# A two-layer transformer kernel on one core: quartered window probes, a fourth PSUM bank for the transposes, and the last attention in sections of two units

## The reference, cut to what matters

```python
h = _layernorm(x) * (1 + ca) + sa            # layer 0
x = x + ga * _L0_attn_ref(h, ...)            # sparse attention, 32 heads of 8, 8 key heads
h = _layernorm(x) * (1 + cb) + sb
x = x + gb * _L0_ffn_ref(h, ...)             # 32 experts, on the first four sequences' tokens
h = _layernorm(x) * (1 + ca) + sa            # layer 1
x = x + ga * _L1_attn_ref(h, ...)            # one attention over 512 tokens with a second softmax
h = _layernorm(x) * (1 + cb) + sb
x = x + gb * _L1_ffn_ref(h, ...)             # RMS norm, causal attention (32 heads of 64), 16 experts
```

## Time and profile before

| | |
|---|---|
| median of 3 runs | 4583.56 us (4581.97 to 4587.42) |
| the profiled execution | 4580.2 us, span 4578.3 us |
| busy share of the span | PE 87%, DVE 69%, PE weight loads 51%, ACT 45%, POOL 33% |
| TensorE clock granted | 0.93 of full speed |
| `phase_a` | to about 1640 us |
| `phase_bc` | 1640 to 2390 us |
| `phase_d` | 2390 to 4060 us |
| `phase_e` | 4060 us to the end |

### The profile page before, as it was taken

The page is one execution under the profiler, slowest core; times in us unless marked ns, Lnnn a source line. Parts: engine busy times, 40 slices in busy tenths (PEclk is TensorE's granted clock), DMA queues, the critical chain, the costliest instruction groups (busy, mean ns, idle before and its releaser), DMA issues.

```text
span 4578.3 us, 83656 instructions
## 1 busy us (share of the span) xinstructions
PE 3971.1 (87%) x28830; PEld 2316.6 (51%) x28831; DVE 3145.4 (69%) x9004; ACT 2061.8 (45%) x4817; POOL 1522.2 (33%) x1291
## 2 busy tenths in 40 slices
PE   6898989899898996998868789898989989859995
PEld 3444445444444444775533344444444444439995
DVE  6777777777777782567746586867677776755555
ACT  1353645353544553332225455555555555534442
POOL 0010101010100102334016465656465655645553
PEclk7899999898999998999989999999999999979998
DMA  5122122221211205862127521212121111145666
GB/s 121 21 33 45 28 41 35 35 37 31 44 31 28 34 15 178 266 205 80 47 67 109 70 64 39 65 41 62 42 61 45 49 58 40 57 152 103 112 106 167
DMA packets 320363, 327.79 MB, mean 72 GB/s; under 512 B 161062, under 2 KB 253630, under 8 KB 318814
## 3 DMA queue, kind: packets, MB, share of 16 engines
q1 hardware_dynamic: 275898, 250.27, 21.7%
q0 software_dynamic: 39936, 70.87, 9.0%
q10 hardware_dynamic: 4112, 1.29, 0.2%
HBM read 182.56 MB, written 92.94 MB: 60 GB/s over the span
## 4 chain that ended last, share of the span: by engine, by line
PE 65%; DVE 23%; ACT 3%; issue 3%; DMA 3%; POOL 2%; SPq 1%; ACTq 0%; DVEq 0%; POOLq 0%
PE PS L2291 7%; PE PS L2813 6%; PE PS L2342 5%; PE PS L2357 4%; PE PS L850 4%; PE PS L2306 3%; DVE a_mm L1246 3%; DVE PS L2624 3%; PE PS L2824 3%; PE PS L790 3%; PE PS L817 3%; PE PS L2326 2%; PE PS L828 2%; PE PS L1754 2%; PE PS L636 2%
## 5 line engine op out<-in xcount | busy, mean ns | idle before, releaser
L1246 DVE TENSOR_REDUCE a_mm<-PS 128x4 f32<-128x512 f32 (+3 forms) x960 | 605.3, 649 | 289.3 <-PE PS L794 253.1
L2698 POOL TENSOR_TENSOR d_ef<-d_ef,d_soft 128x768 f32<-128x768 f32 (+3 forms) x512 | 637.8, 1256 | 356.5 <-DVE d_soft L2633 354.0
L999 ACT ACTIVATE a_PT<-PS 128x512 f32<-128x512 f32 x896 | 512.6, 602 | 503.2 <-PE PS L828 341.5
L2405 ACT ACTIVATE d_ef<-PS,d_soft 128x128 f32<-128x128 f32 (+3 forms) x1024 | 530.3, 525 | 259.5 <-DVE d_soft L2633 192.9
L2624 DVE CUSTOM_DVE_ANT_0 PS<-PS,d_cmask 128x128 f32<-128x128 f32 (+3 forms) x1024 | 481.1, 511 | 219.4 <-PE PS L2326 189.5
L2306 PE MATMUL PS<-W 64*128 64x128 f32 (+3 forms) x2048 | 413.6, 481 | 75.0 <-ACT d_ef L2405 57.5
L2416 ACT ACTIVATE d_tf<-PS 128x512 f32<-128x512 f32 (+1 forms) x384 | 201.9, 526 | 399.2 <-PE PS L2326 398.4
L2342 PE MATMUL PS<-d_tf,W 128*64 128x512 f32 x1280 | 325.6, 641 | 13.8 <-DVE d_tf L2642 13.0
L1453 POOL DMA_INDIRECT list<-a_tok,slots x64 | 63.3, 989 | 817.0 <-ACT a_PT L999 788.6
L2326 PEld LDWEIGHTS PS<-ident,d_ef 64*128 64x128 f32 x5120 | 221.2, 144 | 215.6 <-issue 70.0
L2326 PE MATMUL PS<-ident,d_ef 64*128 64x64 f32 x5120 | 238.8, 231 | 103.3 <-ACT d_tf L2416 47.0
(11 more groups left out here) (389 smaller groups left out, 7873.3 us busy)
## 6 DMA issues: line engine op xcount, KB each, us to landing
W<-W SPq DMA_DIRECT2D x768, 64.0 KB, 2.0
W<-in_exp SPq DMA_DIRECT2D x96, 384.0 KB, 4.8
e_xg<-xrow SPq DMA_DIRECT2D x144, 132.5 KB, 2.1
a_Q<-scr SPq DMA_DIRECT2D x384, 32.0 KB
yrow<-bc_ob SPq DMA_DIRECT2D x48, 256.0 KB, 5.5
W<-in_exp SPq DMA_DIRECT2D x16, 768.0 KB, 10.0
scr<-a_qsp SPq DMA_DIRECT2D x24, 384.0 KB, 3.0
acc<-in_zero POOLq DMA_DIRECT2D x34, 256.0 KB, 11.6
```

The costliest lines, as they stand in the source:

```text
L999: e.activation(PT[:, 4 * (n % 2) + q4, :], RS.of(("exp", n, q4))[:, :], ACT.Exp, scale=S0).then_inc(act.sem, act.mark(("exp", n, q4)))
L1246: e.tensor_reduce(mm[:, i % 2, kind, c:c + len(gs)], RP.of(("top", b, u, kind, gs[0]))[:, 0:len(gs) * n].rearrange("p (g k) -> p g k", g=l ...
L2405: e.activation(ef[:, n % 7, r, 0:nk], S.of(("exp", n))[:, r, 0:nk], ACT.Exp, scale=-1.0, bias=nm[:, n % 7, r:r + 1], accum_out=zz[:, n % 7 ...
L2698: e.tensor_tensor(ef[:, n % 7, :, 0:nk], ef[:, n % 7, :, 0:nk], zr[:, n % 7, :].unsqueeze(2).to_broadcast([128, 2, nk]), ALU.mult).then_in ...
```

## The change

In `phase_a` a window probe is made of four quarters of 32 queries by 96 keys, so its score bank is 384 columns wide. It is issued right behind a `times` where the unit has one. The layer norm takes two instructions for each tile instead of three, in all phases. In `prepare` everything from the transposes of the normed rows on comes two pieces later, on all engines, and a batch has 65 pieces.

In `phase_bc` an empty piece is put behind the second `turn`, and one between the result `o` and its transposes; the steps become 94.

In `phase_d` the bank of `Y` joins the ring `TX`, which has four banks, and `out_proj` takes its bank there. The units are issued in sections of two: first both units' scores, then both turns, both exponentials, and then the product or the output projection; `collect` (line 2650) comes at the start of a section. DVE inverts the sums of two units with one instruction, and POOL scales two units behind it.

```diff
-                e.tensor_scalar(dst[:, i, :], X(4 * b + i), mv[:, i, 0:1], rs[:, 2, i:i + 1], ALU.subtract, ALU.mult
+                e.scalar_tensor_tensor(dst[:, i, :], X(4 * b + i), mv[:, i, 0:1], mb[:, 1, :], ALU.subtract, ALU.mult
...
-                e.tensor_tensor(dst[:, i, :], dst[:, i, :], mb[:, 1, :], ALU.mult).then_inc(dve.sem, dve.tick())
-                chain(e, dve)
-                e.tensor_tensor(dst[:, i, :], dst[:, i, :], mb[:, 0, :], ALU.add
+                e.scalar_tensor_tensor(dst[:, i, :], dst[:, i, :], rs[:, 2, i:i + 1], mb[:, 0, :], ALU.mult, ALU.add
...
-                    want = (2.2 * (u + 1) if u < 15 else 33 + 30 * (u - 14) / 15) if b < 8 else 0
+                    want = (2.2 * (u + 1) if u < 15 else 33 + 32 * (u - 14) / 15) if b < 8 else 0
...
+                    beside = [w[0] for w in order if w[1] is multiply]
+                    for k, w in enumerate(looks):
+                        local = w[3] == 1 and beside
+                        order.append((beside[0] if local else (k + 0.5) / (len(looks) - bool(beside)), *w))
...
-                            for x in range(2):
-                                k0 = 128 * i - 64 + 64 * x
-                                e.matmul(p[64 * x:64 * x + 64, 128 * g:128 * g + 128],
-                                         Q6[0:96, 4 * hh + g, k0 + 64:k0 + 128],
-                                         K6[0:96, y, kind, hh, k0:k0 + 128], start=(g == 0), stop=False)
+                            for x in range(4):
+                                q0 = 128 * i + 32 * x
+                                e.matmul(p[32 * x:32 * x + 32, 96 * g:96 * g + 96],
+                                         Q6[0:96, 4 * hh + g, q0:q0 + 32],
+                                         K6[0:96, y, kind, hh, q0 - 64:q0 + 32], start=(g == 0), stop=False)
...
                     yield from turn(n, 1)
+                    yield
                     turned(n, 1)
...
-            TX = Ring([PS[:, 4, :], PS[:, 5, :], PS[:, 6, :]])
-            Y = PS[:, 7, 0:256]
+            TX = Ring([PS[:, 4, :], PS[:, 5, :], PS[:, 6, :], PS[:, 7, :]])
...
+                for first in (0, *range(1, 9 * N, 2)):
+                    units = (first, first + 1) if first else (first,)
+                    if first >= 13 and first % 4 == 1 and (first - 13) // 4 < 2 * N:
+                        collect((first - 13) // 4)
...
+                    for n in units:
+                        if n < 8 * N:
+                            scores(n)
+                    for n in units:
+                        if n >= 6 and n % 2 == 0 and (n - 6) // 2 < 4 * N:
+                            turn((n - 6) // 2, 1)
+                        if n >= 5 and n % 2 and (n - 5) // 2 < 4 * N:
+                            turn((n - 5) // 2, 0)
+                    for n in units:
+                        if n < 8 * N:
+                            spread(n)
+                    for n in units:
+                        if n >= 10 and n % 4 == 2 and (n - 10) // 4 < 2 * N:
+                            times((n - 10) // 4)
+                        if n >= 12 and n % 4 == 0 and (n - 12) // 4 < 2 * N:
+                            out_proj((n - 12) // 4)
...
-                    if n:
-                        inverse(n - 1)
+                    if n % 2:
+                        inverse(max(n - 2, 0), n - 1)
```

More of the change, by code:

```diff
@@ new lines, in steps @@
+                for first in (0, *range(1, 9 * N, 2)):
+                    units = (first, first + 1) if first else (first,)
+                    if first >= 13 and first % 4 == 1 and (first - 13) // 4 < 2 * N:
+                        collect((first - 13) // 4)
+                    if first < 8 * N:
+                        for n, key in projects:
+                            if n == first:
+                                project(*key)
+                    for n in units:
[14 more added lines that the diff above has]
+                            out_proj((n - 12) // 4)
+                    for n in units:
+                        for b in (n // N - 1, n // N):
+                            if 0 <= b < 8 and n - 64 * (b + 1) in late:
+                                after(*late[n - 64 * (b + 1)], b)
+                        if n < 7 * N and n % N in ahead:
+                            before(*ahead[n % N], n // N + 1)
```

113 lines of the change are left out of this document (47 added, 66 removed).

## The result

The changed kernel takes 4531.8 us (median of 4 runs, 4524.5 to 4540.4) for 4585.5 us before (4 runs): a ratio of 0.988, interval 0.986 to 0.990. That is 54 us faster; the forecast's terms add up to 101 us. The profiled execution has a span of 4528.8 us.

What follows compares the result with a forecast made beforehand. PE was taken as nearest to the bound in every stage touched. Gains of 41 (phase_a), 30 (phase_bc) and 30 us (phase_d), 101 together, took the profiled 4580.2 to 4479, forecast 4482 us as median; range 4405 to 4560.

Steps and rivals of the forecast that it cites:

- The norm: Layer norm, all phases: a tile 0.42 us cheaper on DVE, 18 us of DVE in phase_a, nothing counted in phase_bc and phase_d.
- DVE has room: phase_bc and phase_d: DVE has room, so the cheaper norm counts nothing; if not, a gain of 0.4 us per tile.
- The window probes: phase_a, 192 quartered probes: 0.06 us less each on PE, 12 us, 10 counted; 26 us less on DVE.
- the quarters are bound by issue: Rival in phase_a: sixteen scores take 0.40 us for 0.25, 19 us more in all, total 4511 us; chance 0.15.
- The pieces: phase_a: transposes two pieces later end the 29.3 us of waits at line 273; 20 us counted, extra pieces cost nothing.
- phase_bc: Second half of phase_bc: three PE waits, 38.2 us, get work ahead of them; 30 us gained, bounds 10 and 50.
- phase_d, the ring: phase_d: with four banks transposes no longer wait for copies, bringing 74 us of 1500.
- phase_d, the sections: phase_d: waits of 4.3 us instead of 5.2 in each of 32 turns, ring included, leaving 30 us gained.
- small new waits: Sign of being right in phase_d: small new waits of lines 2350 and 2365 for a bank, 0.3 to 0.6 us each.
- the exponentials become the bound: Rival in phase_d: scores wait for late exponentials, above 140 us; phase_d +109, total 4622 us; chance 0.09.
- The waits only move: Rival: PE comes sooner to the next thing that DVE or ACT is late with, total 4584 us; chance 0.06.
- All of it lands: Rival: each part comes near its upper bound and the clock stays up, 185 us gained, total 4399 us; chance 0.13.

Runs made afterwards that it cites:

- a_spread: The changed kernel with the window probes spread over the unit as before, not right behind the product: 4534.7 us.
- a_later: The changed kernel with the old ramp of 33 + 30 pieces over 15 units instead of 33 + 32, the later transposes kept: 4437.7 us.
- d_units: The changed kernel with phase_d's units in their old order, one at a time, the ring of four banks kept: 4513.5 us.

## Why the prediction was right, and where its sizes were wrong

The sign and the range held, but the gain was half of the forecast's, and in that there was luck: in `phase_a` gains larger than I had counted were cancelled by a loss that I had not, and in `phase_d` two errors of like size met.

**The norm** (18 us of DVE, nothing in `phase_bc` and `phase_d`). An instruction took 485 ns, not the 420 of the earlier trace rows, so it saved 13 us; yet undoing it cost 25 us by the medians (18 + 6 + 9 in the profiles, with the scatter named above). The cover that I named, "DVE has room", was an average: a stage in which DVE is busy for three quarters still has PE waiting for it by name in a dozen places.

**The window probes** (10 us counted of PE's 12, part of 11 of DVE's). They are worth 36 us. The stream got shorter by 0.10 us a probe, my upper bound, for the 0.06 that I took; and up to 0.12 us more may come from the product in front, which the forecast had not seen and a_spread does not bear out. DVE's part, a quarter of 26 us by the forecast, was not seen: PE's waits for maxima are the same with 512 columns. The rival that the quarters are bound by issue fell: 0.18 us from first score to mask, where it put 0.40.

**The pieces** (29.3 us of waits go, 20 counted, "nothing for either" of ramp and placement). This is the step that failed. The waits of line 273 did go, and the shift alone was worth 57 us. But I costed the two more pieces at nothing because they "move no work", and never asked at which half of a unit the chain behind them would come to lie. The two extra pieces of the ramp, not needed for the shift, cost 91 us, nearly all that the norm, the quarters and the shift had brought. The terms of `phase_a` do not add up (norm -18, quarters -36, shift -57, ramp +91 make -20, and it is -3); each was measured with the others in place, and shift and ramp at least depend on one another (the shift brings 57 us with the old ramp and 77 with the new).

**phase_bc** (38.2 - 8 - 5, and 5 for the clock: 30). The three waits did go, but for 3.9 us. The transposes of the next sequence wait now, for DVE's probabilities (19.5 us in 4 waits, up to 4.9), where I had allowed 5, and the scores that moved ahead wait for the copies (8.8 us), which I had not counted. Of the 5 us for the clock little can have come: it is 0.92 from 2020 to 2370 us, for 0.91 before. The shift gave 8 to 11 us, near the lower bound, and the norm 3 to 6 more.

**phase_d, the ring** (74 us with nothing lost). 51 us in the old order. The waits for copies vanished as reckoned, so it is the 74 us that were mis-sized, among them the 0.3 us that I added to each wait from a single pair of rows; 16 us came back as waits for exponentials, 9 as waits of the output projection.

**phase_d, the sections** (44 of the 74 given back, 30 left). 21 given back of 51, 30 left: the sum was right by two errors of like size. The single waits that I listed are there, at 0.5 us for scores, 0.5 for the output projection and 0.4 for the product; "small new waits" was too mild for 48.4 us. A batch was to be 205 us and is 201.5. POOL, at which I counted nothing, takes 19.9 us of PE's time in 10 waits, and stands behind about half of the 21.9 us for `collect` too (six waits of 1.9 to 2.0 us). The rival in which the exponentials become the bound fell: 53.6 us of waiting, where it needed over 140.

**The rivals.** "The waits only move" is what happened in `phase_a`, as a whole, and in none of the other stages. "All of it lands" was not reached by the change, yet a_later, at 4437.7 us, came within 39 us of its 4399: most of the gain was in these edits, and one number, 32 for 30, hid it.

## What to carry to other kernels

When pieces of side work are dealt out over units by a formula, check at which place within a unit each chained step falls before and after, not only how many pieces there are: here a shift of one piece made PE and DVE take turns and cost 47 us, where one of two pieces brought 57. When a change bundles several edits and moves the time little, undo them one at a time; here five gains of 8 to 57 us, the last attention's included, were cut to 54 us by two losses of 91 and 21. A reordering and the buffer that it needs should each be run alone: the fourth bank was the gain, the sections a loss.

## What the runs showed of the hardware

- Scores on four 32-column tiles start one every 11 ns on average (16 in 0.18 us, the row of line 780). From the first matmul of the product, which works on 32-column tiles, to a following group it is 0.88 us for quarters on 32-column tiles and 1.00 us for halves on 64-column tiles.
- PE's waits of 1.43 and 1.85 us were followed by eight projections in 5.4 us instead of 3.7, one of 1.66 us by the same eight in 3.8. The wait of 1.85 us and the 1.7 us behind it make about twice what its row shows, an estimate from this one place; the granted clock there was 0.69, behind the wait of 1.66 us it was 1.00, and over that quarter of a batch 0.86 for 0.91. That the wait brought the clock down is not shown.
- The same DVE instruction takes longer while POOL scales. The second of the norm's two took 485 ns in `phase_a` (POOL busy for 138 of 1500 us) and 1975 ns on average in `phase_d` (874 of 1470). In `phase_d` of the changed kernel:

```profile
L244 DVE SCALAR_TENSOR_TENSOR f_y<-f_y,rs,mb 128x256 f32<-128x256 f32 x24 | 47.4, 1975 | 0.9
```

  The mean hides two kinds: of the 24, twelve took 485 ns, six 2.59 us and six 4.34 us. The long ones are those in which a scaling of line 2710 begins; the rows at 2908.80 and 2909.11 show one of 4.34 us, which ends 0.3 us behind two scalings, and those of 2.59 us end 0.3 us behind one. In the kernel before the norm's first instruction (line 239) took 2.20 us at one place of each batch, beside the scaling of line 2698. The norm's first instruction in the changed kernel (line 241) has none beginning in it, and took 485 ns. In d_units, where POOL scales one unit at a time, it is line 241 that meets a scaling, and takes 1.8 to 2.2 us at one place of each of these batches.
